# Plain and transposed attention scores in the two row halves of one array

## The reference

```python
x = x + _L0_attn_ref(_layernorm(x), Wqkv, Wout)          # 16 heads of 8, causal
x = x + _L0_ffn_ref(_layernorm(x), centroids, ...)       # top 2 of 8 experts, 128 -> 512 -> 128
x = x + _L1_attn_ref(_layernorm(x), Wq, bq, ...)         # 16 query heads, one key/value head, rotary
x = x + _L1_ffn_ref(_layernorm(x), w_gate, w_up, w_down) # fp4-quantized gated unit, inner width 352

# both attentions, per batch element and head (q, k, v: 512 x 8)
attn = einsum('qd,kd->qk', q, k) / sqrt(8)
attn = softmax(where(causal, attn, -inf))
out = attn @ v
```

## Time and profile before

| what | us |
|---|---|
| median of three runs | 696.56 |
| the profiled execution | 694.38 |
| its span, first to last instruction | 692.7 |
| TensorE matmuls busy | 569.9 |
| VectorE busy | 476.6 |
| ScalarE busy | 337.0 |
| GpSimd busy | 222.5 |

### The profile page before, as it was taken

The page is one execution under the profiler, slowest core; times in us unless marked ns, Lnnn a source line. Parts: engine busy times, 40 slices in busy tenths (PEclk is TensorE's granted clock), DMA queues, the critical chain, the costliest instruction groups (busy, mean ns, idle before and its releaser), DMA issues.

```text
span 692.7 us, 12790 instructions
## 1 busy us (share of the span) xinstructions
PE 569.9 (82%) x4419; PEld 386.9 (56%) x4470; DVE 476.6 (69%) x1171; ACT 337.0 (49%) x646; POOL 222.5 (32%) x224
## 2 busy tenths in 40 slices
PE   3586999899887869889986898588979999986565
PEld 1443566665544338778965665345646565454444
DVE  4689677759875525765556657767867877647993
ACT  2022667667666724435533241436656676763221
POOL 6411010222234322460554025422030103254664
PEclk9999999999999989999999899889999999999885
DMA  8527796856321131222324004203012100000001
GB/s 257 138 75 158 169 240 146 177 122 128 65 61 44 42 101 32 62 75 57 89 54 111 27 17 128 56 22 95 25 37 85 49 25 27 27 0 1 15 17 30
DMA packets 51294, 53.43 MB, mean 77 GB/s; under 512 B 6975, under 2 KB 44081, under 8 KB 51201
## 3 DMA queue, kind: packets, MB, share of 16 engines
q1 hardware_dynamic: 49185, 48.42, 27.5%
q0 software_dynamic: 2048, 4.20, 2.2%
HBM read 33.56 MB, written 21.10 MB: 79 GB/s over the span
## 4 chain that ended last, share of the span: by engine, by line
PE 36%; DVE 18%; POOL 4%; issue 3%; ACT 3%; DMA 1%; SPq 1%; POOLq 0%; DVEq 0%; ACTq 0%
PE ps L630 5%; PE ps L1245 5%; DVE mx L826 4%; PE ps L611 4%; PE ps L587 4%; PE ps L1233 2%; PE ps L656 2%; PE ps L590 2%; ACT pT L713 1%; PE ps L614 1%; PE ps L1224 1%; DVE xn L1139 1%; PE ps L1226 1%; PE ps L1227 1%; PE ps L1225 1%
## 5 line engine op out<-in xcount | busy, mean ns | idle before, releaser
L826 DVE TENSOR_REDUCE mx<-ps 128x2 f32<-128x1024 f32 (+2 forms) x192 | 196.0, 1040 | 64.3 <-PE ps L590 63.1
L713 ACT ACTIVATE pT<-ps 128x512 f32<-128x512 f32 x320 | 182.8, 596 | 54.0 <-PE ps L614 50.7
L590 PE MATMUL ps<-mask_qk,identb 128*128 128x128 bf16 (+2 forms) x352 | 87.1, 248 | 3.6 <-DMA stB<-max_scratch 1.1
L614 PE MATMUL ps<-mask_kq,identb 128*128 128x128 bf16 (+1 forms) x320 | 81.3, 254 | 4.4 <-issue 2.6
L630 PE MATMUL ps<-pT,vA 128*32 128x512 f32 (+3 forms) x1024 | 77.0, 435 | 1.4 <-ACT pT L713 1.4
L611 PE MATMUL ps<-stB,kA 128*128 128x384 bf16 (+3 forms) x241 | 56.2, 302 | 11.6 <-ACT pT L713 11.1
L587 PE MATMUL ps<-kA,stA 128*128 128x384 bf16 (+3 forms) x245 | 54.6, 304 | 8.7 <-DVE mx L826 8.4
L587 PE MATMUL ps<-stA 128*128 128x384 bf16 (+3 forms) x247 | 55.1, 303 | 6.9 <-DVE mx L826 3.7
L611 PE MATMUL ps<-stB 128*128 128x384 bf16 (+3 forms) x240 | 55.6, 299 | 5.6 <-ACT pT L713 4.4
L630 PEld LDWEIGHTS ps<-pT,vA 128*32 128x32 f32 x1024 | 39.9, 110 | 31.4 <-issue 20.7
L1269 ACT ACTIVATE pT<-ps 128x512 f32<-128x512 f32 x46 | 27.4, 596 | 61.2 <-PE ps L1227 61.1
(11 more groups left out here) (296 smaller groups left out, 1114.5 us busy)
## 6 DMA issues: line engine op xcount, KB each, us to landing
stA<-stack_scratch SPq DMA_DIRECT2D x48, 192.0 KB, 3.3
stB<-stack_scratch SPq DMA_DIRECT2D x48, 192.0 KB, 4.0
stack_scratch<-part SPq DMA_DIRECT2D x12, 384.0 KB, 3.1
stack_scratch<-part SPq DMA_DIRECT2D x12, 256.0 KB, 3.1
pairs_scratch<-b1r SPq DMA_DIRECT2D x46, 64.0 KB
pT<-pairs_scratch SPq DMA_DIRECT2D x46, 64.0 KB, 1.9
outs_scratch<-pT SPq DMA_DIRECT2D x46, 64.0 KB
w_lo<-w_scratch SPq DMA_DIRECT2D x8, 256.0 KB, 4.0
```

The costliest lines, as they stand in the source:

```text
L590: last = pe.matmul(diagonal, identb[:], mask_qk[:].unsqueeze(1).broadcast_to([P, per, P]), start=False, stop=True)
L614: last = pe.matmul(blocks, identb[:], mask_kq[:].unsqueeze(1).broadcast_to(blocks.shape), start=False, stop=True)
L713: act.activation(dst_, src, ACT.Exp, scale=SCALE).then_inc(a["ex"], 1)
L826: nc.vector.tensor_reduce(mx[:, g % 2, qb, heads[0]:heads[0] + nh], src, AX.X, ALU.max).then_inc(a["maxd"], 1)
```

## The change

There is now one stack, st, of 128 rows: the plain operands in rows 0..47 of it, the transposed ones in rows 64..111 with their maxima in 112..114. Plain products contract over rows 0..63 alone and transposed ones over rows 64..127, so that each takes half of the array's rows. A mask has 128 rows, which a contraction over 64 can't carry at once: it is added in two matmuls, the first with the identity's rows of that half over the full block, the second with identx (the identity with its halves exchanged) over 64 of the block's columns. kA, rk, wkr, wks, pick_sb and the bias columns hold a second copy of layer 1's key in rows 64..111, so K's steps work on 112 rows, and rk and pick_sb are loaded by six DMAs in place of two.

A new step PAIR issues one slot's matmuls on TensorE. A slot has one plain unit and one or two transposed ones (BESIDE); side_by_side merges the matmuls of both by the number of columns that stand ahead of each on its side. The other engines still see S and ST, behind the slot's PAIR. The small steps keep their places between the slots. LOADA and LOADB write their rows of st. FP4's tmp_h has memory of its own. GpSimd's clear of stB is gone.

```diff
-MR = SR
-KR = P
+HI = P // 2
+MR = HI + SR
...
+def plain_parts(u):
+    qb, heads = S_UNITS[u]
+    w = (qb + 1) * P
+    per = 512 // w
+    return [(c, m, (w,) * per + (per * P, per * HI)) for c in range(len(heads) // per) for m in range(per + 2)]
+def turned_products(u):
+    if u >= 2 * HG:
+        return [(2 * (u - 2 * HG) + m, 2, m * 256) for m in range(2)]
+    return [(u // 2, 1, 0), (u // 2, 3, 384)] if u % 2 else [(u // 2, 0, 0)]
+def turned_parts(u):
+    products = turned_products(u)
+    blocks = 1 if len(products) == 1 else 2
+    widths = tuple(T - kb * P for _, kb, _ in products) + (blocks * P, blocks * HI)
+    return [(m, widths) for m in range(len(widths))]
+BESIDE = [((0,), (0,)), ((1,), (1, 2)), ((2,), (3,)), ((3,), (4, 5)), ((4,), (6, 7)), ((5,), (8, 9))]
+def side_by_side(slot):
+    steps = []
+    ahead = 0
+    for u in BESIDE[slot][0]:
+        for c, m, widths in plain_parts(u):
+            steps.append((ahead, 0, ("S", u, c, m)))
+            ahead += widths[m]
+    ahead = 0
+    for u in BESIDE[slot][1]:
+        for m, widths in turned_parts(u):
+            steps.append((ahead, 1, ("ST", u, 0, m)))
+            ahead += widths[m]
+    return [step for _, _, step in sorted(steps)]
...
-            def scores(*units):
-                return [(n, s, g, u) for u in units for n in ("S",) + ("WARM",) * warm(layer, s, g) if s < B]
-            def turned_scores(*units):
-                return [("ST", s - 1, g, u) for u in units if 1 <= s <= B]
+            def scores(slot):
+                o = [("PAIR", s, g, slot)] * (s <= B)
+                o += [("S", s, g, u) for u in BESIDE[slot][0] if s < B]
+                o += [("ST", s - 1, g, u) for u in BESIDE[slot][1] if 1 <= s <= B]
+                return o + [("WARM", s, g, slot)] * warm(layer, s, g)
             def between(v):
...
-            o += between(0) + scores(0) + turned_scores(0) + scores(1) + turned_scores(1) + between(1)
-            o += turned_scores(2) + scores(2) + between(2) + turned_scores(3, 4) + scores(3) + between(3)
-            o += turned_scores(5) + scores(4) + turned_scores(6) + between(4)
-            o += turned_scores(7) + scores(5) + turned_scores(8) + between(5) + turned_scores(9)
+            o += between(0) + scores(0) + scores(1) + between(1) + scores(2) + between(2)
+            o += scores(3) + between(3) + scores(4) + between(4) + scores(5) + between(5)
...
+        identx = sb("identx", [P, P], BF16)
...
-        stA_all = sb("stA", [P, 2, 2 * HG, T], BF16)
-        stA = stA_all[0:KR]
-        stB = sb("stB", [KR, 2, 2 * HG, T], BF16)
+        st = sb("st", [P, 2, 2 * HG, T], BF16)
...
+        tmp_h = sb("tmp_h", [P, 2, 2, 2 * I])
...
-                st, ld, used, per = (stA, "loadA", "sc", NS) if name == "LOADA" else (stB, "loadB", "st", NV)
+                row, ld, used, per = (0, "loadA", "sc", NS) if name == "LOADA" else (HI, "loadB", "st", NV)
...
+        def plain_scores(pe, layer, b, g, u, c, m):
             a = A[layer]
-            i = b * G + g
-            if name == "S":
-                qb, heads = S_UNITS[u]
-                n = i * NS + u
+            qb, heads = S_UNITS[u]
+            n = (b * G + g) * NS + u
+            w = (qb + 1) * P
+            per = 512 // w
+            bank = score_pair(layer, n) + c
+            if c == 0 and m == 0:
                 if u == 0:
-                    pe.wait_ge(cleared, 3)
+                    pe.wait_ge(cleared, 2)
+                    pe.wait_ge(made, 8)
                     pe.wait_ge(loads["loadA"][g], loaded(layer, b))
                     if layer:
                         pe.wait_ge(a["kacc"], b + 1)
@@ -578,20 +621,29 @@
                     pe.wait_ge(M["ge"], HALVES * NTL)
                 elif n >= 2:
                     pe.wait_ge(a["maxd"], n - 1)
-                w = (qb + 1) * P
-                pair, per = score_pair(layer, n), 512 // w
-                for m, j in enumerate(heads):
-                    h = (g % 2) * HG + j
-                    bank, at = pair + m // per, m % per * w
-                    kk = stA[:, 1, h, :] if layer == 0 else kA[:, b, :]
-                    pe.matmul(ps[:, bank, at:at + w], stA[:, 0, h, qb * P:w], kk[:, 0:w], start=(at == 0), stop=False)
-                    if m % per == per - 1:
-                        diagonal = ps[:, bank, 0:per * w].rearrange("p (h k) -> p h k", k=w)[:, :, w - P:w]
-                        last = pe.matmul(diagonal, identb[:], mask_qk[:].unsqueeze(1).broadcast_to([P, per, P]),
-                                         start=False, stop=True)
-                last.then_inc(a["sc"], 1)
-            elif name == "ST":
-                n = i * NV + u
+            diagonal = ps[:, bank, 0:per * w].rearrange("p (h k) -> p h k", k=w)[:, :, w - P:w]
+            if m < per:
+                h = (g % 2) * HG + heads[c * per + m]
+                kk = st[0:HI, 1, h, :] if layer == 0 else kA[0:HI, b, :]
+                pe.matmul(ps[:, bank, m * w:(m + 1) * w], st[0:HI, 0, h, qb * P:w], kk[:, 0:w], start=(m == 0), stop=False)
+            elif m == per:
+                pe.matmul(diagonal, identb[0:HI, :], mask_qk[0:HI, :].unsqueeze(1).broadcast_to([HI, per, P]),
+                          start=False, stop=False)
+            else:
+                last = pe.matmul(diagonal[:, :, HI:P], identx[0:HI, :],
+                                 mask_qk[0:HI, 0:HI].unsqueeze(1).broadcast_to([HI, per, HI]), start=False, stop=True)
+                if (c + 1) * per == len(heads):
+                    last.then_inc(a["sc"], 1)
+        def turned_scores(pe, layer, b, g, u, m):
+            a = A[layer]
+            i = b * G + g
+            n = i * NV + u
+            products = turned_products(u)
+            bank = ps[:, ST_BANK[n % 2], :]
+            if m == 0:
                 if u == 0:
                     pe.wait_ge(loads["loadB"][g], loaded(layer, b))
                     pe.wait_ge(loads["mload"][g], 16 * (B * layer + b + 1))
@@ -601,19 +653,30 @@
                         pe.wait_ge(M[read], HALVES * NTL)
                 if n >= 2:
                     pe.wait_ge(a["ex"], n - 1)
-                bank = ps[:, ST_BANK[n % 2], :]
-                todo = ([(u // 2, 0, 0)], [(u // 2, 1, 0), (u // 2, 3, 384)])[u % 2] if u < 2 * HG else [
-                    (2 * (u - 2 * HG) + m, 2, m * 256) for m in range(2)]
-                for j, kb, at in todo:
-                    h = (g % 2) * HG + j
-                    w = T - kb * P
-                    kk = stB[:, 1, h, :] if layer == 0 else kA[:, b, :]
-                    last = pe.matmul(bank[:, at:at + w], kk[:, kb * P:(kb + 1) * P], stB[:, 0, h, kb * P:T],
-                                     start=(at == 0), stop=False)
-                blocks = diagonal_blocks(bank, u)
-                last = pe.matmul(blocks, identb[:], mask_kq[:].unsqueeze(1).broadcast_to(blocks.shape),
-                                 start=False, stop=True)
-                last.then_inc(a["st"], 1)
+            blocks = diagonal_blocks(bank, u)
+            if m < len(products):
+                j, kb, at = products[m]
+                h = (g % 2) * HG + j
+                w = T - kb * P
+                kk = st[HI:P, 1, h, :] if layer == 0 else kA[HI:P, b, :]
+                pe.matmul(bank[:, at:at + w], kk[:, kb * P:(kb + 1) * P], st[HI:P, 0, h, kb * P:T], start=(m == 0), stop=False)
+            elif m == len(products):
+                pe.matmul(blocks, identb[HI:P, :], mask_kq[HI:P, :].unsqueeze(1).broadcast_to([HI] + list(blocks.shape[1:])),
+                          start=False, stop=False)
+            else:
+                part_ = blocks[:, :, 0:HI]
+                pe.matmul(part_, identx[HI:P, :], mask_kq[HI:P, HI:P].unsqueeze(1).broadcast_to([HI] + list(part_.shape[1:])),
+                          start=False, stop=True).then_inc(a["st"], 1)
+        def attention_tensor(pe, take, layer, name, b, g, u):
+            a = A[layer]
+            i = b * G + g
+            if name == "PAIR":
+                for kind, unit, c, m in side_by_side(u):
+                    if kind == "S" and b < B:
+                        plain_scores(pe, layer, b, g, unit, c, m)
+                    elif kind == "ST" and b:
+                        turned_scores(pe, layer, b - 1, g, unit, m)
...
-            elif name == "CLEAR":
-                nc.gpsimd.memset(stB[:].rearrange("p c h t -> p (c h t)"), 0.0).then_inc(cleared, 1)
...
-            sp.dma_start(rk[:], rope_k.rearrange("c p t -> p c t")).then_inc(ld_w1, 16)
-            sp.dma_start(pick_sb[:], pick).then_inc(ld_w1, 16)
+            for row, n in ((0, SR), (SR, HI - SR), (HI, SR)):
+                sp.dma_start(rk[row:row + n], rope_k[:, 0:n].rearrange("c p t -> p c t")).then_inc(ld_w1, 16)
+                sp.dma_start(pick_sb[row:row + n], pick[0:n]).then_inc(ld_w1, 16)
...
+            for at in (0, HI):
```

(2 more changed lines are left out.)

88 lines of the change are left out of this document (42 added, 46 removed).

## The result

| | us |
|---|---|
| before, median of 4 runs beside it | 696.39 (695.63 to 697.1) |
| after, median of 4 runs | 722.69 (719.21 to 725.33) |
| ratio, 95% interval | 1.0373 [1.0335, 1.0412] |

The account below looks back on a forecast made before the run. TensorE's stream was taken to bound the paired groups, with VectorE next. From 694.4 us, 18 off in paired groups and 5 on in unpaired rounds gave 681.4, as a median 683.5 us; range 667 to 704.

Parts of the forecast that it names:

- What bounds the kernel now: Paired rounds: TensorE's stream bounds the 10.36 us groups; VectorE is next, about 1.9 us a group behind at best.
- What the change takes away: Score products and masks of a paired group: both halves stream at once, 3.89 us instead of 5.97, 2.08 us off TensorE.
- The changes of shape: TensorE switching between half and whole array: about 0.10 us each, 5.5 a paired group, 0.55 us added.
- rival 2: Paired groups: row halves don't overlap, TensorE gets 2048 more columns (0.85 us) a group; 735 us, chance 0.10.
- rival 3: TensorE: each change of shape drains and refills the array for more than 0.10 us; 714 us, chance 0.08.
- What comes next: Walk through one paired group, TensorE against VectorE: 9.6 us instead of 10.36, 0.75 us a group, 18 us in all.
- VectorE's wait for scores halves from 2 us to 1: Sign expected in the trace after, in steady paired groups of 9.6 us.
- rival 4: Slots: a wait for a reduction or exponential holds both sides, 0.3 us lost a slot, groups stay at 10.4; 701 us, chance 0.13.
- That the clock falls is no case of its own: Paired stretches: clock stood at 0.99 and 0.96, and TensorE would still be busy some 8.8 of 9.6 us.
- Unpaired rounds: Rounds 0 and 4, one half unused: second masks and changes of shape add 5 us together, bounds 1 and 14.
- Edits at nothing: Added DMA issues, dropped memset, identx copies, K's 112 rows, FP4's temporary: no cost; 2.6 us if SP's idle time didn't cover the loads.
- Sum: Whole kernel: 694.4 - 18 + 5 = 681.4 us for the profiled execution, 683.5 as a median.

Follow-up runs that it names:

- e18: Kernel before, with VectorE's row maxima and (from each layer's third group) ScalarE's exponentials cut to a quarter of their columns: ratio 0.96.
- e14: e6 with VectorE's row maxima and ScalarE's exponentials both cut to a quarter of their columns: 653.0 us, ratio 0.9376.
- e6: Changed kernel, two stacks, halves and slots only in paired rounds 1 to 3, rk and pick_sb loads behind the w_scratch copy: 697.6 us, ratio 0.9997.
- e10: e6 with only VectorE's row maxima cut to a quarter of their columns: 9.8 us a clean group, from a single run.
- e13: e6 with only ScalarE's exponentials cut to a quarter of their columns, from each layer's third group on: ratio 0.9871, 9.6 us a clean group.
- e4: Kernel before, with WARM's 72 idle matmuls over 64 rows instead of 128: 702.2 us, ratio 1.0079.
- e7: Control: changed kernel with two stacks again, GpSimd's clear and FP4's temporary as before, halves in all rounds: 725.0 us, ratio 1.0397.
- e1: Changed kernel with two stacks, unpaired rounds 0 and 4 at all 128 rows with one mask, halves only in paired rounds: 701.8 us, ratio 1.0082.

## Why the prediction was wrong

**What bounds the kernel now: half right.** TensorE's stream was the bound, but with little room above it. With both other engines relieved (e18) the four groups take 39.3 us instead of 41.5, so 9.8 us of the 10.4 are the stream at most, and the rest was already spent on the others. "VectorE is next" named one of the two that are next.

**What the change takes away: right in kind, too large in size. The changes of shape: right.** Halves overlap (against rival 2), and a change of shape costs 0.10 us (against rival 3). TensorE's stream was forecast at 8.8 us a group and e14 has 8.9, but that is luck: two errors cancel. It was 10.36 - 2.08 + 0.55; measured with both other engines relieved it is 9.8 - 1.4 + 0.5. The runs of score products and masks take 6.00 us a group in e18 and 4.58 in e14, so 1.4 us go and not 2.08; all else of a group grows from 3.8 to 4.3. In these kernels halves are worth 0.9 us a group, and 13.7 us in the paired rounds of both layers (121.8 + 120.1 against 114.2 + 114.0). Even this is under the 18 of the sum.

**"What comes next", the walk: this step failed.** It followed TensorE and VectorE and left ScalarE out, because it is busy only 6.9 us a group. A share of busy time was the wrong ground. In a slot two transposed units come at once, and a slot of 1600 columns would last 0.67 us (slot 1 of the clean group below takes 0.93, from 582.12 to 583.05); the two banks behind it are free only after two exponentials of 0.6 us each, 1.2 us. ScalarE's timeline in e6 shows four units in a row at that pace, after 1.07 us of idleness, and the wait for PV's result ahead of it:

```profile
564.29 0.60 ACT L845 ACTIVATE oT<-ps 128x512 f32<-128x512 f32 x1 [1.61 <-PE ps L721]
...
566.44 2.34 ACT L804 ACTIVATE pT<-ps 128x512 f32<-128x512 f32 x4 [1.07 <-PE ps L690]
```

ScalarE, like VectorE, idles while MT, PV and OT hold TensorE and then has to make it up in the slots.

Both sides of a slot are held by one wait, and the kernel after shows two ways. TensorE and ScalarE in slots 0 and 1 of a clean group:

```profile
582.09 0.60 ACT L776 ACTIVATE pT<-ps 128x512 f32<-128x512 f32 x1 [0.44 <-PE ps L668]
582.17 0.22 PE L668 MATMUL ps<-mask_kq,identx 64*128 64x128 bf16 x1
582.42 0.38 PE L628 MATMUL ps<-kA,st 64*128 64x512 bf16 x1
582.74 0.39 PE L662 MATMUL ps<-st,kA 64*128 64x512 bf16 x1
582.74 0.23 PE L630 MATMUL ps<-mask_qk,identb 64*128 64x128 bf16 x1
582.85 1.08 ACT L776 ACTIVATE pT<-ps 128x512 f32<-128x512 f32 x2 [0.16 <-PE ps L668]
```

The transposed product L662 has to wait for the exponential that ends at 582.69, and the plain mask L630 behind it, whose own product had streamed by 582.64, starts only with it. And the transposed unit that L668 closes at 582.39 is signalled only at 582.82, when the plain product L628 is over (582.80), so ScalarE starts at 582.85. L628 stands ahead of it in TensorE's list and yet starts after it (582.42 against 582.17). By the trace's semaphore events all 40 transposed units of the last four clean groups are signalled 15 ns or less after the end of their last record before; after, 22 of the 40 come later than 22 ns, by 0.5 us a group in sum and 0.44 us at most. The eight that are over 0.1 us late all come with the end of a plain product. What this costs was not tested by itself. The forecast was 9.6 us a group; the four clean ones take 10.1, and e10 (9.8) and e13 (9.6) show that neither engine alone is the reason. The predicted sign "VectorE's wait for scores halves from 2 us to 1" did not come: 9.7 us over five groups against 10.3. The mechanism is rival 4's (an exponential or a reduction holds both sides of a slot), the argument against which was the same busy share. Its time of 701 us is not what came; it had no loss in the unpaired rounds beyond the 5 us and none of the clock. Its sign, groups that stay at 10.4 us, came only in part.

The Trainium skill ("TensorEngine Tiling (Array Packing)", PSUM Bottleneck) warns that tiling speeds up TensorE but not what empties PSUM, and advises to use both engines for that. The trace agrees, and sharper: here both do, each for its own side, and with either one relieved the other keeps the group within 0.3 to 0.5 us of where it was.

**"That the clock falls is no case of its own": this sentence failed.** It was argued from TensorE's busy time. In clean groups halves win 0.3 us (layer 1) to 0.5 us (layer 0's first), which over 24 would be 7 to 12 us, less than the forecast but a gain; by the account of e6 the drops take it back. Low-clock time rose from 59 to 126 us in the profiled executions, and from 3.4 to 30.8 in the two paired stretches, which had stood at 1.00 and 0.99. The argument didn't hold: in e4, with the same count and columns of matmuls and half the rows in 72 of them, the full clock comes 6.8 us later after the first product, and the total is 5.9 us longer.

**Unpaired rounds: 5 us forecast (bounds 1 and 14), 23 measured (e7 less e1).** The terms counted, 0.43 us of second masks and 0.3 to 0.5 of changes a half group, don't reach. At the start and in layer 0's round 4 the clock is missing from the sum (previous point): 12.1 us of that round are low, none before. In layer 1's round 4 it is little: 3.4 us are low, 1.7 us at most, and the stage is 7.2 us longer, 1.8 us a group where 0.7 was forecast, while the order of slots costs only 0.5 of the 7.2 (e1: 42.2). How the rest splits between masks, changes and ScalarE's banks stays open.

**Edits at nothing: one was not.** "SP ends that one's issue at 11.95 and is next needed at 17.95" looked at the queue that issues; what moved was the transfer. The cover was right for SP and missing for the DMA engines, behind the w_scratch copy: 1.8 us at the first product, against the 2.6 named "without that cover". The memset and tmp_h show no cost: e7, which has both as before, and after agree within their scatter. identx and K's 112 rows are in all kernels with halves and were not tested by themselves.

**Sum.** In the profiled executions 18 gained where 4.5 were lost, and 5 lost where 26 were, the 1.8 of the loads among them: 681.4 + 22.5 + 21 = 724.9, against 725.05 measured (the median is 722.7). One bound of the prediction was summed wrong and bore on nothing here: 1.9 us over 24 groups is 46 us, not 38.

## What to carry to other kernels

Before an engine's stream is shortened, cut the work of each other engine in turn, and of all at once, and read what a step would then take. Here e18, an edit of the kernel before, shows 9.8 us of the 10.4 a group to be TensorE's at most, and e14, the same edit with halves, 8.9: the shorter stream can bring 0.9 us a group at best, and 0.3 with the other two as they are. Where two units come out at once and the consumer has buffers for two in all, its mean share says nothing of whether it keeps up; more banks or a slot with one transposed unit were not tried. And use half the array only where the other half is filled: a half-height matmul alone has the same columns, here needed its masks twice, and in e4 the full clock came later with it.

## What the runs showed of the hardware that was not expected

- Full clock came later with half-height matmuls: with 72 idle matmuls over 64 rows instead of 128 it began 9.9 us after the first product in place of 3.1 (e4), and with half-height products too 15.5 us after it (after). In the paired stretches low clock was 3.4 us before and 23.9 in e6, but 3.4 also in e14, which has e6's half-height products with both other engines relieved.
- Even with full-height matmuls it falls: in the kernel before there are 59 us of low clock, among them 69.4 to 72.8 and 250.3 to 257.1 us.
- One row half can run ahead of the other, but it isn't signalled ahead of it: a unit that ended at 582.39 was signalled at 582.82, with the end of the other half's product that stands before it in the list. Before, all 40 units looked at were signalled 13 to 15 ns after their end.
- The clock column of a window is 1.00 where no record exists; at the start only the spacing of matmuls (0.16 against 0.30 us after a product of 384 columns) tells the level.
- A large copy from memory to memory held the stores issued 4 us and more behind it: its packets ended 1.84 us later, those of the stores 1.86, and their reader started 1.82 us later.
